# A new work order for a fused attention and gated feed-forward kernel, with a changed first batch: 1/sigma ahead on GpSimd, the first rotation on VectorE, selectors behind the stacks, feed-forward weights asked for early

## The reference, cut to what matters

```python
x = L0_attn_x                               # (8, 512, 256) float32
xn = (x - mean) / sqrt(var + 1e-5)          # over the last axis
q, k, v = xn @ wq + bq, xn @ wk + bk, xn @ wv + bv   # 16 heads of 16
q, k = rope(q), rope(k)                     # pairs (even, odd) rotated by position
scores = q k^T / 4 + causal mask;  attn = softmax(scores)
s = (attn v) @ wo + bo
wg, wu, wd = int32 weights * (1/127)        # 768 hidden
g = silu((silu(xn @ wg.T) * (xn @ wu.T)) @ wd.T)
return x + s * g
```

## Time and profile before

| | us |
|---|---|
| median of three runs | 558.88 |
| lowest, highest | 558.67, 562.95 |
| the profiled execution, its own time | 564.23 |
| its span, first to last instruction | 562.5 |
| PE busy in it | 506.4 (90%) |
| DVE busy | 461.9 (82%) |
| ACT busy | 332.2 (59%) |
| POOL busy | 292.6 (52%) |
| mean granted TensorE clock | 0.965 of full |

### The profile page before, as it was taken

One profiled execution on the slowest core, in us unless ns is written; L12 is line 12 of the kernel. 1 busy time (PEld: TensorE's weight loads), 2 busy tenths in 40 slices (PEclk: granted clock), 3 DMA queues, 4 the chain that ended last, 5 costly groups with the idle time before them and its releaser, 6 DMA issues.

```text
span 562.5 us, 11714 instructions
## 1 busy us (share of the span) xinstructions
PE 506.4 (90%) x3717; PEld 349.5 (62%) x3717; DVE 461.9 (82%) x1460; ACT 332.2 (59%) x682; POOL 292.6 (52%) x407
## 2 busy tenths in 40 slices
...
GB/s 194 183 157 241 120 71 140 116 98 166 67 4 197 196 65 115 116 176 109 108 123 145 195 63 115 149 182 110 134 101 151 113 173 115 128 124 60 4 77 38
DMA packets 47839, 69.47 MB, mean 124 GB/s; under 512 B 5496, under 2 KB 22776, under 8 KB 47776
## 3 DMA queue, kind: packets, MB, share of 16 engines
q1 hardware_dynamic: 46688, 67.62, 45.7%
...
## 4 chain that ended last, share of the span: by engine, by line
PE 66%; DVE 15%; issue 5%; DMA 5%; SPq 4%; ACT 2%; POOL 2%; ACTq 0%; DVEq 0%; POOLq 0%
PE ps_w L544 36%; PE ps_w L556 15%; PE ps_o L648 10%; DVE ps_w L877 8%; PE ps_w L657 2%; SPq L517 2%; SPq L501 1%; DMA gate<-L_attn_wo 1%; ACT probs L767 1%; DVE row_max L877 1%; PE ps_w L663 1%; PE ps_w L569 1%; DMA k_st<-parts_k 1%; DVE high_low L865 1%; DVE hid L910 1%
## 5 line engine op out<-in xcount | busy, mean ns | idle before, releaser
L877 DVE CUSTOM_DVE_ANT_0 ps_w<-ps_w,cst 128x512 f32<-128x512 f32 (+3 forms) x512 | 235.3, 520 | 20.3 <-PE ps_w L556 19.4
L767 ACT ACTIVATE probs<-ps_w 128x512 f32<-128x512 f32 (+1 forms) x384 | 179.8, 535 | 63.8 <-PE ps_w L556 62.5
L959 POOL TENSOR_SCALAR_AFFINE_SELECT probs<-probs 128x256 f32<-128x256 f32 x256 | 108.5, 439 | 170.2 <-ACT probs L767 169.3
L544 PE MATMUL ps_w<-xt_hi,wgu_hi 128*128 128x512 f32 x192 | 84.1, 438 | 2.6 <-DVE row_max L877 1.1
L648 PE MATMUL ps_o<-probs,vals 128*32 128x512 f32 (+3 forms) x1024 | 84.6, 444 | 0.1
L556 PE MATMUL ps_w<-k_st,q_st 48*128 48x512 f32 (+3 forms) x512 | 80.0, 363 | 3.9 <-DMA k_st<-parts_k 1.8
L556 PE MATMUL ps_w<-q_st,k_st 52*128 52x512 f32 (+3 forms) x512 | 76.9, 354 | 4.4 <-DMA q_st<-minus_max 2.9
L544 PE MATMUL ps_w<-xt_lo,wgu_hi 128*128 128x512 f32 x192 | 76.8, 400 | 0.0
L556 PEld LDWEIGHTS ps_w<-k_st,q_st 48*128 48x128 f32 x512 | 45.0, 188 | 43.4 <-issue 28.1
L877 DVE DVE_READ_ACCUMULATOR2_ANT row_max<- 128x1 f32 x512 | 71.4, 139 | 0.0
L556 PEld LDWEIGHTS ps_w<-q_st,k_st 52*128 52x128 f32 x512 | 44.7, 187 | 32.4 <-issue 14.8
...
## 6 DMA issues: line engine op xcount, KB each, us to landing
parts_q<-high_low SPq DMA_DIRECT2D x48, 256.0 KB, 3.1
...
parts_k<-high_low SPq DMA_DIRECT2D x42, 256.0 KB, 3.1
...
q_st<-minus_max SPq DMA_DIRECT2D x256, 4.0 KB
...
```

The lines of the kernel that those rows point to most:

```text
L544: last = pe.matmul(dst, w, m, start=(i == 0), stop=(i == len(terms) - 1))
L767: nc.scalar.activation(probs[:, (pair % 2) * SLOTS + slot, col:col + WIDTH[c]], w_of(kind, b, 3 * pair + c // 2, c % 2)[:, 0:WIDTH[c]], AC ...
L877: last = nc.vector.tensor_tensor_reduce(out=ps[:, col:col + w], in0=ps[:, col:col + w], in1=cst[:, C_MASK + SEQ - w:C_MASK + SEQ], scale=1 ...
L959: nc.gpsimd.affine_select(out=v, in_=v, compare_op=ALU.is_ge, fill=0.0, base=0, pattern=[[0, 2], [1, P]], channel_multiplier=-1).then_inc( ...
```

## The change: what it does

1. ACT: WO.0 (rounding wo) moves from ahead of WQ to behind G1.0. POOL: WC.0 (low part of wo) moves from ahead of RS.0 to behind B0.0; RS.0 comes first. wv gets a semaphore of its own, so that WQ's first two roundings wait for wq and wk alone.
2. All twelve RP steps of batch 0 stand in DVE's list. RP of batch 1 starts POOL's rotations, and RS.1 waits until all four LO of batch 0 are done (`lo_ready` 4). The four memsets (WQ.0 on DVE) come after XT.0 in place of first.
3. SL.0 of SP moves behind RD3.0. The rounded selectors lie in `at_hi` in place of `h_hi`; the first AT step of ACT waits for their DMAs in place of the first HL.
4. FL.0 of SP moves ahead of XL.1, which waits for XT.0; so the feed-forward weights are asked for right behind the constants. RL0.0 moves from ahead of RD0.0 to behind WS1.1, and waits for all 12 rotations.
5. PE takes QK0 to QK3 of batch 0 ahead of V0; G0, G1, U0 and U1 of batch 0 ahead of A0.0. All five lists are in a new order throughout, with other PSUM banks. The number of steps of each kind and batch is the same, except for the three RP steps that change engines.

The lists, cut to the first batch and to the last lines (the rest differs in the same manner):

```diff
 "sp":
-  ID0.0 XL0.0 CL0.0 XL0.1 FL0.0 SL0.0 WS0.0 WS1.0 WS2.0 WS3.0 RL0.0 RD0.0 RD1.0 RD2.0 RD3.0 XL0.2 MD0.0 WS0.1 WS1.1 WS2.1 MD1.0
+  ID0.0 XL0.0 CL0.0 FL0.0 XL0.1 WS0.0 WS1.0 WS2.0 WS3.0 RD0.0 RD1.0 RD2.0 RD3.0 SL0.0 MD0.0 XL0.2 WS0.1 MD1.0 WS1.1 RL0.0 WS2.1
...
-  WS1.2 MD0.1 RD3.1 MD1.1 MD2.1 WS2.2 WS3.2 RD0.2 RD1.2 MD3.1 RD2.2 ST0.0 XL0.4 RL0.1 MD0.2 RD3.2 MD1.2 WS0.3
+  WS1.2 WS2.2 MD2.1 WS3.2 RD0.2 MD3.1 ST0.0 RD1.2 RD2.2 XL0.4 MD0.2 WS0.3 RL0.1 RD3.2 MD1.2 WS1.3 WS2.3
...
 "pe":
-  WU0.0 XT0.0@0 XT1.0@1 WU1.0 V0.0@2 QK0.0@3 QK1.0@4 QK2.0@5 QK3.0@6 V1.0@0 WT0.0@1 WT1.0@2 WT2.0@3 WT3.0@4 WT4.0@5 WT5.0@6
-  MX0.0@0 WT6.0@1 FLAG0.0 WT7.0@0 WT8.0@2 WT9.0@3 WT10.0@4 A0.0@56 G0.0@1 A1.0@02 G1.0@5 G2.0@6 U0.0@0 A2.0@21 G3.0@3 G4.0@4
+  WU0.0 XT0.0@0 XT1.0@1 WU1.0 QK0.0@2 QK1.0@3 QK2.0@4 QK3.0@5 V0.0@6 WT0.0@0 WT1.0@1 WT2.0@2 WT3.0@3 WT4.0@4 WT5.0@5 V1.0@0
+  WT6.0@1 WT7.0@2 WT8.0@6 WT9.0@3 MX0.0@0 WT10.0@4 FLAG0.0 G0.0@5 G1.0@0 U0.0@1 U1.0@2 A0.0@63 A1.0@45 G2.0@0 G3.0@1 U2.0@2 U3.0@6
+  U4.0@3 A2.0@04 A3.0@15 G4.0@2 U5.0@0 A4.0@64 G5.0@1 XT0.1@5 XT1.1@6 A5.0@24 MT0.0@5 A6.0@24 V0.1@6 A7.0@52 QK0.1@4 QK1.1@1
+  A8.0@36 A9.0@45 V1.1@0 A10.0@12 B0.0@36
...
-  DN1.7@4 B23.7@56 ON2.7@0 PV12.7 PV13.7 PV14.7 PV15.7 ON3.7@3 AT1.7@1 OP0.7@2 OP1.7@5
+  DN1.7@3 ON2.7@2 B23.7@41 PV12.7 PV13.7 PV14.7 PV15.7 ON3.7@0 AT0.7@6 AT1.7@5 OP0.7@2 OP1.7@4
 "act":
-  WL0.0 WO0.0 WQ0.0 XT0.0 XT1.0 SL0.0 QK0.0 QK1.0 QK2.0 QK3.0 HI0.0 HI1.0 HI2.0 HI3.0 WC0.0 WC1.0 SQ0.0 SQ1.0 WC2.0 SQ2.0 WT0.0
+  WL0.0 WQ0.0 XT0.0 XT1.0 QK0.0 SL0.0 QK1.0 QK2.0 HI0.0 QK3.0 WC0.0 HI1.0 WC1.0 WC2.0 HI2.0 WT0.0 WT1.0 HI3.0 SQ0.0 WT2.0 WT3.0
+  WT4.0 SQ1.0 SQ2.0 WT5.0 WT6.0 WT7.0 WT8.0 WT9.0 WT10.0 G0.0 G1.0 WO0.0 HL0.0 HL1.0
...
 "dve":
-  WQ0.0 ST0.0 WC0.0 NM0.0 NM1.0 NM2.0 NM3.0 XT0.0 XT1.0 V0.0 RP0.0 ST0.1 RP1.0 RP2.0 RP6.0 RP7.0 LO0.0 RP8.0 RP9.0 RP10.0 RP11.0
-  LO1.0 LO2.0 LO3.0 V1.0 SQ0.0 WT0.0 MX0.0 WT1.0
+  ST0.0 NM0.0 NM1.0 NM2.0 NM3.0 WC0.0 XT0.0 XT1.0 WQ0.0 RP0.0 RP1.0 RP2.0 RP3.0 RP4.0 RP5.0 RP6.0 LO0.0 RP7.0 LO1.0 RP8.0 RP9.0
+  RP10.0 RP11.0 LO2.0 ST0.1 LO3.0 WT0.0 WT1.0 WT2.0 V0.0 WT3.0 V1.0 WT4.0 SQ0.0 WT5.0 MX0.0 WT6.0
...
 "pool":
-  WQ0.0 WC0.0 RS0.0 RS0.1 RP3.0 RP4.0 RP5.0 NM0.1 NM1.1 NM2.1 NM3.1 RP0.1 RP1.1 RP2.1 RP3.1 RP4.1 RS0.2 B0.0 RP5.1
+  WQ0.0 RS0.0 RS0.1 NM0.1 NM1.1 NM2.1 NM3.1 RP0.1 RP1.1 RP2.1 B0.0 WC0.0 B1.0 RP3.1 RP4.1 RP5.1 RS0.2
```

The rest of the diff:

```diff
@@ -335,7 +335,7 @@
         ps_o = ctx.enter_context(nc.psum_tensor("ps_o", [P, SEQ], F32))
         ps_w = [ctx.enter_context(nc.psum_tensor(f"ps_w{i}", [P, SEQ], F32)) for i in range(WORK_BANKS)]
 
-        ... w3_in = sem("w3_in"); wo_in = sem("wo_in"); ffn_w_in = sem("ffn_w_in"); x_in = sem("x_in")
+        ... w3_in = sem("w3_in"); wv_in = sem("wv_in"); wo_in = sem("wo_in"); ffn_w_in = sem("ffn_w_in"); x_in = sem("x_in")
         sel_in = sem("sel_in"); sel_rounded = sem("sel_rounded"); sel_set = sem("sel_set")
         res_in = sem("res_in"); out_stored = sem("out_stored")
         full = {"act": sem("work_full_for_act"), "dve": sem("work_full_for_dve")}
@@ -384,10 +384,8 @@
         def rope_at(b, t, n):
 
             if b:
-                return rope_done, 3 + 6 * (2 * (b - 1) + t) + n
-            if t == 0 and n > 3:
-                return rope_done, n - 3
-            return start_rope_done, 3 * t + n
+                return rope_done, 6 * (2 * (b - 1) + t) + n
+            return start_rope_done, 6 * t + n
 
         def h_lo_at(b, i):
 
@@ -439,11 +437,7 @@
                 tensor_tensor(turned, even, sin if e else cos, ALU.mult).then_inc(done, 1)
             elif part == 1:
                 need(eng, raw_ready, 2 * n + 2)
-                if n == 1 and not e:
-                    need(eng, *rope_at(0, 0, 3))
-                elif n == 2 and not e:
-                    need(eng, *rope_at(0, 0, 6))
-                elif e and n:
+                if e:
                     need(eng, *rope_at(b, t, 3))
                 elif n:
                     need(eng, *rope_at(b if t else b - 1, 1 - t, 6))
@@ -481,11 +475,11 @@
                     for a in range(2):
                         for g in range(GROUPS):
                             sp.dma_start(k_st[64 * a + STACK:64 * a + STACK + 4, 2 * g:2 * g + 2, :].bitcast(F32),
-                                         h_hi[4 * a:4 * a + 4, 0:2, :].bitcast(F32)).then_inc(sel_set, 16)
+                                         at_hi[4 * a:4 * a + 4, :, :].bitcast(F32)).then_inc(sel_set, 16)
                 elif kind == "RL":
                     need(sp, out_stored, 16 * b)
                     if b == 0:
-                        sp.wait_ge(start_rope_done, 9)
+                        sp.wait_ge(start_rope_done, 12)
                     sp.dma_start(res[:], by_tile(x[b])).then_inc(res_in, 16)
                 elif kind == "ST":
                     need(sp, res_ready, 2 * (b + 1))
@@ -707,21 +701,21 @@
             def do(kind, b, i):
                 if kind == "WL":
                     for j, w in enumerate((wq, wk, wv)):
-                        act.dma_start(w3_raw[:, :, j * DM:(j + 1) * DM], w.rearrange("(t p) d -> p t d", p=P)).then_inc(w3_in, 16)
+                        act.dma_start(w3_raw[:, :, j * DM:(j + 1) * DM], w.rearrange("(t p) d -> p t d", p=P)).then_inc(wv_in if j == 2 else w3_in, 16)
                     act.dma_start(wo_raw, wo.rearrange("(t p) d -> p t d", p=P)).then_inc(wo_in, 16)
                 elif kind == "WQ":
                     act.wait_ge(w3_in, 32)
                     for k in range(KT):
                         nc.scalar.copy(w3_hi[:, k, 0:2 * DM].rearrange("p (t e m) -> p t e m", t=2, e=2),
                                        w3_raw[:, k, 0:2 * DM].rearrange("p (t m e) -> p t e m", t=2, e=2)).then_inc(w3_hi_ready, 1)
-                    act.wait_ge(w3_in, 48)
+                    act.wait_ge(wv_in, 16)
                     nc.scalar.copy(w3_hi[:, :, 2 * DM:], w3_raw[:, :, 2 * DM:]).then_inc(w3_hi_ready, 1)
                 elif kind == "WO":
                     act.wait_ge(wo_in, 16)
                     nc.scalar.copy(wo_hi[:], wo_raw).then_inc(wo_hi_ready, 1)
                 elif kind == "SL":
                     act.wait_ge(sel_in, 16)
-                    nc.scalar.copy(h_hi[0:SELECTORS, 0:2, :], hid[0:SELECTORS, :, :]).then_inc(sel_rounded, 1)
+                    nc.scalar.copy(at_hi[0:SELECTORS, :, :], hid[0:SELECTORS, :, :]).then_inc(sel_rounded, 1)
                 elif kind == "WC":
                     act.wait_ge(ffn_w_in, 48)
                     nc.scalar.copy(w_nat[:, i, :], w_nat[:, i, :].bitcast(I32)).then_inc(ffn_w_float, 1)
@@ -772,6 +766,8 @@
                     nc.scalar.copy(o_t[:, :], ps_o[:, :]).then_inc(o_t_ready, 1)
                 elif kind == "AT":
                     wait_full(act, kind, b, i)
+                    if b == 0 and i == 0:
+                        act.wait_ge(sel_set, 16 * 2 * GROUPS)
                     nc.scalar.copy(at_hi[:, i, :], w_of(kind, b, i)[:, :]).then_inc(at_hi_ready, 1)
                 elif kind == "G":
                     wait_full(act, kind, b, i)
@@ -785,8 +781,6 @@
                                          scale=0.5 * WSCALE).then_inc(tanh_ready, 1)
                 elif kind == "HL":
                     need(act, hid_ready, b * HT + i + 1)
-                    if b == 0 and i == 0:
-                        act.wait_ge(sel_set, 16 * 2 * GROUPS)
                     if b == 0 and i == 2:
                         act.wait_ge(part_written[0], 96)
                         act.wait_ge(part_written[1], 96)
@@ -935,6 +929,8 @@
                     pool.wait_ge(half_set, 1)
                 elif kind == "RS":
                     need(pool, xn_ready, TT * b)
+                    if b == 1:
+                        pool.wait_ge(lo_ready, 4)
                     need(pool, aggr_ready, TT * (b + 1))
                     nc.gpsimd.tensor_scalar(rstd[:], mean_var[:, :, 1], EPS, None, ALU.add).then_inc(rstd_ready, 1)
                     need(pool, rstd_ready, 2 * b + 1)
@@ -944,7 +940,7 @@
                 elif kind == "NM":
                     normalise(pool, nc.gpsimd.tensor_scalar, b, i)
                 elif kind == "RP":
-                    if b == 0 and i == 3:
+                    if b == 1 and i == 0:
                         pool.wait_ge(const_in, 16)
                     rotate(pool, nc.gpsimd.tensor_tensor, b, i, rope_t[:])
                 elif kind == "HL":
```

267 lines of the change are left out of this document (133 added, 134 removed).

## The result

The changed kernel took 542.21 us (median of four runs, 535.34 to 551.12); the kernel before, run beside it, 558.77 (558.35 to 562.95). By these medians it is faster by 16.6 us, where 11.5 were forecast. The ratio, 0.961 with a 95% interval of 0.950 to 0.973, compares fast runs alone, of which the changed kernel has two here (535.34 and 540.89), and so it stands for some 21.6 us. The changed kernel's first profile is of its slowest run (551.12), so sums are made with the profile of e1, an execution of 541.41 with a span of 539.5.

The account below looks back on a forecast made before the run. TensorE was taken to bound a full body, after a start of 53.9 us in which it does little. 564.23 - 5.35 (episode) - 12.9 (start) + 0.5 (tail) + 0.9 (body) = 547.4 us, range 541.5 to 555.

Parts of the forecast that it names:

- the start: First 53.9 us, in which TensorE does little: G0 was to begin at 41.0, 12.9 us earlier.
- Body: The full middle stretch: 2.9 us of idleness in 240, some 5 us in all to win; a loss of 0.9 taken.
- the episode: A TensorE wait and low clock around 240 to 260 us of the profiled execution, 5.35 us, taken as absent from median runs.
- Tail: The end of the kernel: AT0.7 no longer fills a gap, a loss of 0 to 1.3 us, 0.5 taken.
- ScalarE's own list sets the time: Start, feed-forward weights: they land by 17, so ScalarE's biases, roundings, squares and WT fix G0 at 41.0.
- The cover of 2.3 us: Start: G0, G1, U0 and U1 take 6.7 us, so the first A at 47.7 comes behind the stack at 45.4.
- Step 2: Batch 0's rotation all on VectorE: 2.1 us added, no operation drawn out from 0.69 to 1.74, last LO at 33.5.
- Step 3: Key stacks on SP's queue: first stack at 45.4; the selectors, hidden before, stay hidden behind RD3 until 59.2 at the latest.
- (a): Rival: the body gets better too, by up to 5 us, giving 542.5; chance 0.13.
- (b): Rival: VectorE becomes the bound behind the start and 5 of the 12.9 us go, giving 552.4; chance 0.15.
- (c): Rival: ScalarE holds up a LO or wv comes late, so half the start's gain goes, 554 to 557; chance 0.08.
- (d): Rival: MD steps caught in SP's queue cost 5.3 us each; slower, 568 for 4 of 8 batches; chance 0.06.

Follow-up runs that it names:

- e1: The changed kernel as it is, timed again in six more runs: 541.86 us, 0.969 of the kernel before.
- e14: The changed kernel plus, behind its last output product, matmuls on old data with array shapes grouped or in turn; its time isn't to be compared.
- e5: The changed kernel with 22 pairs of neighbours swapped in PE's list, 43 changes of shape more: 554.46 us, 0.991 of the kernel before.
- e6: The kernel before with 22 pairs of neighbours swapped in PE's list, 41 changes of shape more: 576.19 us, 1.027 of the kernel before.
- e3: The kernel before up to MT0.1 of PE, from there on the order of the changed kernel: 561.58 us, 1.004 of the kernel before.
- e9: The changed kernel with wo's rounding back ahead of WQ on ScalarE and its low part ahead of RS.0 on GpSimd: G0 3.4 us later.
- e13: The changed kernel with ScalarE's first list put back as it was before, roundings and squares behind the last HI: 0.979 of the kernel before.

## Why the prediction was wrong, step by step

The direction and the large term, the start, were right; the size was short by 5.5 us (547.4 against 541.9), and so the likeliest case of the forecast was not the one that came.

- **Body, the step that failed.** "The body's order is new, but it has 2.9 us of idleness in 240 to win, some 5 us in all" took TensorE's busy time as fixed, because no matmul is removed. It isn't: own work fell by 4.0 us (3.0 to 4.1 by the way of summing). The list has 42 changes of shape fewer, and e14 shows that a change costs 0.17 to 0.20 us of busy time. That would be 7 to 8 us, twice what was gained, so not every change pays the full price, or the new order loses something elsewhere. e5, e6 and e14 show that changes cost busy time; that the fewer changes are what gave the 4.0 is argued from them, not shown. The same sentence also looked at 260 to 500 alone: the 5.1 us that the kernel before loses from 500 to 520 were there to win, and the new order won them. It lost some 7 elsewhere, in three places that e3 shows too. So the forecast loss of 0.9, where 2.1 were measured without the episode, was near by luck: it is the difference of two parts that the working didn't have.
- **Tail.** Forecast +0.5, measured -1.5. Idleness is 0.7 less, and the clock took 0.8 less. Its cause was not followed and stays open.
- **Start, 14.1 for 12.9.** 1/sigma ended at 9.6, not 10.3, since its two operations took 0.23 and 1.04 in place of 0.67 and 1.33. The weights' low parts took 1.28 for two, not 2.00; GpSimd did nothing beside them, and in e9, where wo's low part was made before them, they took 1.29. The first bias came at 17.5 for 18.7, the last LO at 32.0 for 33.5, G0 at 38.7 for 41.0. So "ScalarE's own list sets the time" was the right reading, and e13 shows that it is the heaviest of all, 7.2.
- **The cover of 2.3 us wasn't there.** "16 matmuls of 0.42, 6.7 us" took the distance at 1.2 GHz from the start of the kernel before. At 38.7 TensorE soon ran at full clock: the last of the 16 starts at 42.54, 3.82 / 15 = 0.25 us from start to start, 4.1 us in all. The stack landed at 45.4, just as forecast, and so TensorE waits 2.5 us for it (0.5 in e1, where it landed earlier). First A at 45.4 or 43.5 in place of 47.7.
- **Step 2** is worth 0.4 at G0, as small as the working had it (2.1 more on VectorE against operations drawn out). **Step 3**: the selectors were hidden before and would have been in front of WS too; right. **wo's low part** behind B0: nothing waits for it.
- **Rivals.** (a), a better body, gave the time nearly to the microsecond (542.5), but by luck: it was to come out of idleness, and the body's idleness and clock without the episode got worse. (b) in part: its sign was VectorE over 95% and TensorE under 93% from 41 to 80, and e1 has 36.81 and 35.96 of 39 us, 94% and 92%; but the 5 us that it was to cost are not in the start, which gained more than forecast. (c) no. (d) MD was caught in no batch, but SP's queue does matter for x. In the first profile this row stands in the chain that ended last, issued by SP right behind 16 others that it began at 289.44:

```profile
299.17 8.14 DMA xn<-L_attn_x
```

  The load of x lands at 307.3, VectorE has stood 2.9 us with the statistics behind it, and TensorE then waits 1.87 us for a row maximum. In e1 the same load took 7.00 and began at 295.94, and VectorE still stood 2.07 us, TensorE 1.03. So this stall belongs to the new order, and differs little between the two runs (5.2 us lost from 280 to 320 against 4.3). Of the 7.9 us between their bodies 6.0 lie from 400 to 480; what made them, and the spread from 535 to 551, stays open.
